# A two-layer graph network on one core: the inverse root of the degrees is taken by ScalarE, from VectorE's inverse counts, straight into the output rows

## What is computed

```python
h = jnp.maximum(_layernorm(x), 0.0)                   # x is 100000 x 128
neigh = h[dst] @ W_neigh.T + b_neigh                  # edge_index = (src, dst), 125000 edges
agg, count = segment_sum(neigh, src), clip(segment_sum(ones, src), 1)
x = x + h @ W_self.T + b_self + agg / count[:, None]  # layer one
h = jnp.maximum(_layernorm(x), 0.0)
deg = segment_sum(ones, dst)
dis = where(deg > 0, deg ** -0.5, 0)
x = x + relu(segment_sum(h[src] * (dis[src] * dis[dst])[:, None], dst))   # layer two
```

## Time and profile before

| | |
|---|---|
| time, median of 3 runs | 1208.86 us (1208.85, 1208.86, 1210.57) |
| profiled execution: span from first to last instruction | 1206.2 us |
| busy share of the span | PE 71%, PEld 65%, DVE 86%, ACT 88%, POOL 73% |
| layer one | from the first gather at about 28 us to the last store, issued at 717.7 us |
| layer two | from its first gather at 721.6 us to the end |
| mean granted TensorE clock | 0.779 |

### The profile page before, as it was taken

One profiled execution on the slowest core, in us unless ns is written; L12 is line 12 of the kernel. 1 busy time (PEld: TensorE's weight loads), 2 busy tenths in 40 slices (PEclk: granted clock), 3 DMA queues, 4 the chain that ended last, 5 costly groups with the idle time before them and its releaser, 6 DMA issues.

```text
span 1206.2 us, 30367 instructions
## 1 busy us (share of the span) xinstructions
PE 856.0 (71%) x9408; PEld 782.6 (65%) x9408; DVE 1042.0 (86%) x2896; ACT 1059.9 (88%) x2774; POOL 874.6 (73%) x1145
## 2 busy tenths in 40 slices
PE   1389999999999999999899972444444444444444
PEld 1378999998989998899899971343343433334334
DVE  7789999988989999999898845888888888888886
ACT  2489999998999999999899955888888888888886
POOL 4777777777777777777777507777777777777771
PEclk6699999999999999999999995555555555555555
DMA  5336667666766676677667435888888889888884
GB/s 206 116 85 200 200 211 212 189 193 203 207 193 196 206 212 188 198 204 213 179 205 210 143 115 185 255 262 272 267 265 280 259 268 275 264 283 256 263 280 185
DMA packets 82230, 259.38 MB, mean 215 GB/s; under 512 B 19986, under 2 KB 20356, under 8 KB 82116
## 3 DMA queue, kind: packets, MB, share of 16 engines
q1 hardware_dynamic: 58948, 210.86, 55.1%
q0 software_dynamic: 22400, 46.91, 14.5%
q10 hardware_dynamic: 768, 0.20, 0.1%
HBM read 152.93 MB, written 104.37 MB: 213 GB/s over the span
## 4 chain that ended last, share of the span: by engine, by line
POOL 48%; issue 25%; PE 9%; ACT 7%; DVE 6%; DMA 3%; POOLq 2%; ACTq 0%; DVEq 0%
POOL X L678 39%; ACT work L788 4%; POOL work L631 3%; POOL work L635 3%; PE p_O L962 2%; PE p_O L974 2%; DMA X<-in_x,IDX 2%; DVE ST L1397 2%; POOL work L615 2%; PE p_T L937 1%; PE p_T L912 1%; DVE area L1459 1%; POOL factor L651 1%; ACT area L803 1%; ACT p_O L788 1%
## 5 line engine op out<-in xcount | busy, mean ns | idle before, releaser
L788 ACT ACTIVATE work<-X,shift,scale 128x128 f32<-128x128 f32 x1323 | 546.9, 512 | 2.0 <-DVE shift L1434 1.8
L678 POOL DMA_INDIRECT X<-in_x,IDX x392 | 389.4, 993 | 128.2 <-issue 100.7
L1397 DVE BATCH_NORM_STATS2 ST<-X 128x6 f32<-128x256 f32 x1176 | 408.6, 414 | 37.6 <-DMA X<-in_x,IDX 35.6
L1025 PE MATMUL p_O<-work 32*128 32x128 f32 x1984 | 205.3, 435 | 223.9 <-POOL work L619 142.7
L678 POOL DMA_INDIRECT X<-x_table,IDX x294 | 286.0, 973 | 93.3 <-issue 90.5
L1025 PEld LDWEIGHTS p_O<-work 32*128 32x128 f32 x1984 | 178.0, 323 | 244.4 <-issue 186.2
L788 ACT ACTIVATE p_O<-X,shift,scale 128x128 f32<-128x128 f32 x496 | 201.3, 444 | 27.0 <-DVE area L1490 24.1
L962 PE MATMUL p_O<-wnT,area 128*128 128x128 f32 x1568 | 216.9, 282 | 2.9 <-DVE area L1459 2.9
L974 PEld LDWEIGHTS p_O<-wsT,area 128*128 128x128 f32 x1568 | 206.8, 192 | 7.5
L974 PE MATMUL p_O<-wsT,area 128*128 128x128 f32 x1568 | 207.4, 275 | 0.0
L962 PEld LDWEIGHTS p_O<-wnT,area 128*128 128x128 f32 x1568 | 191.6, 193 | 3.9 <-DVE area L1459 3.8
(11 more groups left out here) (177 smaller groups left out, 1163.3 us busy)
## 6 DMA issues: line engine op xcount, KB each, us to landing
x_table<-area SPq DMA_DIRECT2D x98, 528.0 KB
X<-x_table SPq DMA_DIRECT2D x98, 528.0 KB
X<-in_x SPq DMA_DIRECT2D x98, 512.0 KB, 4.6
out_x<-area SPq DMA_DIRECT2D x98, 512.0 KB, 5.9
X<-in_x,IDX POOLq DMA_INDIRECT x392
X<-x_table,IDX POOLq DMA_INDIRECT x294
moved<-held SPq DMA_DIRECT2D x32, 12.2 KB
es<-in_src SPq DMA_DIRECT2D x1, 488.5 KB, 3.4
```

Source lines behind the costliest of these rows:

```text
L678: nc.gpsimd.indirect_dma_start(got(s)[:, k, 0:w], None, table, bass.IndirectOffsetOnAxis(ap=IDX[:, s, k:k + 1], axis=0)).then_inc(gathered ...
L788: last = nc.scalar.activation(o, row(l, s, r), ACT.Relu, bias=shift[:, s, r:r + 1], scale=scale[:, s, r:r + 1])
L1025: ends[half] = nc.tensor.matmul(outs1[p][g][:, c], SEL[1][q, p, part_of, :], H[1][q, p, draw, :], start=False, stop=(half == 1 and part_of ...
L1397: last = V.bn_stats(ST[:, s, r:r + 2, :].rearrange("p r k -> p (r k)"), pair.rearrange("p r c -> p c r"))
```

## The change

DVE's inverse counts `rc` are kept for five blocks instead of two, and `sdeg` is gone. ACT, at the place in its step where the root of the counts was, now takes the root of `rc` of a block two blocks older, and writes it into column 128 of that block's output rows (`dis`, semaphore `dis_ready`). For this it waits for the store of two blocks before. PE's `aggregate` now waits for DVE's `counts_read`. DVE's second inverse is gone; SP waits for DVE's last L1459 and for `dis_ready`.

```diff
-        rc = sb("rc", [P, 2, BT])
-        sdeg = sb("sdeg", [P, HT, BT])
+        rc = sb("rc", [P, HT, BT])
...
-                sp.wait_ge(y_ready[l], place(l, turn, old)[0] + 1)
+                if l == 0:
+                    sp.wait_ge(prod_used[1], old + 1)
+                    sp.wait_ge(dis_ready, old + 1)
+                else:
+                    sp.wait_ge(y_ready, place(l, turn, old)[0] + 1)
...
-            def root_degrees(turn, off):
+            def dis(turn, off):
+
                 i, _, _ = place(0, turn, off)
                 act.wait_ge(counts_read, i + 1)
-                nc.scalar.activation(sdeg[:, off % HT, :], p_c[:, 0:BT], ACT.Sqrt).then_inc(sdeg_ready, 1)
+                if not first(i, HR[0]):
+                    act.wait_ge(stored[0][off % HR[0]], stores_before(0, turn, off) * 16)
+                nc.scalar.activation(made(0, off % HR[0])[:, :, D].rearrange("p (g j) -> p g j", g=2),
+                                     rc[:, off % HT, :].rearrange("p (j g) -> p g j", g=2), ACT.Sqrt
+                                     ).then_inc(dis_ready, 1)
...
-                if there(0, turn, off - 1):
-                    root_degrees(turn, off - 1)
+                if there(0, turn, off - 3):
+                    dis(turn, off - 3)
...
-                    pe.wait_ge(sdeg_ready, i)
+                    pe.wait_ge(counts_read, i)
...
-                    pe.wait_ge(sdeg_ready, NB)
+                    pe.wait_ge(counts_read, NB)
...
-            def dis(turn, off):
-
-                i, s, _ = place(0, turn, off)
-                dve.wait_ge(sdeg_ready, i + 1)
-                V.reciprocal(made(0, off % HR[0])[:, :, D].rearrange("p (g j) -> p g j", g=2),
-                             sdeg[:, off % HT, :].rearrange("p (j g) -> p g j", g=2)).then_inc(y_ready[0], 1)
...
                 dve.wait_ge(aT_ps, i + 1)
-                V.reciprocal(rc[:, off % 2, :], p_c[:, 0:BT]).then_inc(counts_read, 1)
+                if not first(i, HT):
+                    dve.wait_ge(dis_ready, i - HT + 1)
+                V.reciprocal(rc[:, off % HT, :], p_c[:, 0:BT]).then_inc(counts_read, 1)
...
                     added(turn, off - 3, 1)
-                    dis(turn, off - 3)
```

More of the change, by code:

```diff
@@ L161, in schedule, with stores_before @@
             step(0, off)
+    def stores_before(l, turn, off):
+        return turn * (RING[l] // HR[l]) + off // HR[l]
     def group_of(i):
@@ L414, in gnn @@
         h_ready = [sem(f"h_ready{l}") for l in range(2)]
-        y_ready = [sem(f"y_ready{l}") for l in range(2)]
+        y_ready = sem("y_ready1")
         hT_ps = sem("hT_in_psum")
@@ L420, in gnn @@
         counts_read = sem("counts_read")
-        sdeg_ready = sem("sqrt_deg_ready")
+        dis_ready = sem("dis_columns_ready")
         n_ready = [sem(f"neighbour_products_ready{g}") for g in range(2)]
@@ L777, in normalise @@
                         if l == 1:
-                            act.wait_ge(y_ready[1], i - HR[1] + 1)
+                            act.wait_ge(y_ready, i - HR[1] + 1)
                 if l == 1 and first(i, HR[1]) and i == HR[1] - 1:
@@ L1448, in scaled @@
                 bank = out0(off, g)[:, :].rearrange("p (a b) -> p a b", a=GT)
-                V.tensor_tensor(bank, bank, rc[:, off % 2, g:BT:2].rearrange("p (a b) -> p a b", b=1).to_broadcast([P, GT, P]),
+                V.tensor_tensor(bank, bank, rc[:, off % HT, g:BT:2].rearrange("p (a b) -> p a b", b=1).to_broadcast([P, GT, P]),
                                 ALU.mult).then_inc(n_scaled[g], 1)
@@ L1460, in added @@
                                 own(0, s)[:, GT * g:GT * g + GT, 0:D], ALU.add).then_inc(prod_used[g], 1)
-            def dis(turn, off):
-                i, s, _ = place(0, turn, off)
-                dve.wait_ge(sdeg_ready, i + 1)
-                V.reciprocal(made(0, off % HR[0])[:, :, D].rearrange("p (g j) -> p g j", g=2),
-                             sdeg[:, off % HT, :].rearrange("p (j g) -> p g j", g=2)).then_inc(y_ready[0], 1)
-            def stores_before(l, turn, off):
-                return turn * (RING[l] // HR[l]) + off // HR[l]
             def inverse_counts(turn, off):
@@ L1492, in finish1 @@
                 if g == 1:
-                    last.then_inc(y_ready[1], 1)
+                    last.then_inc(y_ready, 1)
             def step0(turn, off):
```

## The result

The changed kernel takes 1212.13 us (median of 20 runs, 1209.15 to 1214.5) against 1208.26 us for the kernel before (20 runs, 1206.54 to 1211.95). The ratio is 1.0026, 95% interval 1.0019 to 1.0034: slower, by 2.3 to 4.1 us. I had forecast no measurable change.

The account below looks back on a forecast made before the run. POOL's pace, 6.72 us a block, was taken to bound layer one, hiding most of the change; 0.43 us off its end took the median from 1208.86 to 1208.4 us, range 1205 to 1211.7.

Parts of the forecast that it names:

- the rival that came true: Layer one: DVE's new phase puts L1418 on POOL's L631; six more blocks cost 2.6 us, typical loss 3 us; chance 0.12.
- The sign that I had set for being wrong: POOL, layer one: L631's mean or L678's gaps changing by over 25 ns a block, or ACT waiting for stores.
- the sum: End of layer one: 0.21 + 0.11 + 0.11 = 0.43 us off, nothing else on the path.
- PE's start 0.14 us behind the inverse's end: Last wait before POOL's last gathers end: PE follows DVE's inverse by the same 0.14 us as it followed ACT's root.
- the 0.21: End of layer one: PE waits for DVE's inverse instead of ACT's root and starts 0.21 us sooner.
- the first 0.11 us: Behind the last gathered rows that hold DVE up: without the second inverse, the inverse of rows 8 comes 0.11 us sooner.
- the second 0.11: Very end of layer one: no inverse behind the last L1459, so the last store goes out 0.11 us sooner.
- ACT's 15.5 us in front of the root: Layer one: ACT's wait for DVE's inverse, 17 places; forecast to vanish there, most of it idle elsewhere on ACT.
- the 0.5 us that I expected: End of layer one: ACT's last root waits for a store, delaying the `DISL` DMAs some 0.5 us; cost 0.
- The inverse, put at 0.11 us a block: DVE, steady part: dropping the second inverse saves 0.11 us a block, hidden; 10.8 us for all 98 were DVE the bound.
- ACT's root out of SBUF: ACT, steady part: the root reading SBUF costs 0.13 us more a block, hidden under POOL's pace.
- the inverse's removal gives POOL nothing: Port rule: L1418 and L1434 contend with POOL, the removed inverse never did, so its removal alone gives POOL nothing.

Follow-up runs that it names:

- e5: Changed kernel plus one DVE inverse of `rc` into a spare tile where the removed one was; 1211.72 us, ratio 1.0000 to the kernel before.
- e6: Changed kernel with the old waits back: ACT's root for the newest counts, PE's `aggregate` for ACT's root; 1214.65 us, ratio 1.0026 to the kernel before.
- e7: Changed kernel with POOL's normalising instructions moved between the second and third gather, one step earlier; 1193.71 us, ratio 0.9858 to the kernel before.
- e8: Kernel before with POOL's normalising instructions moved between the second and third gather, one step earlier; 1190.39 us, ratio 0.983 to the unmoved kernel before.

## Why the prediction was wrong

**The step that failed** is in the rival that came true, where I argued against it: "A DVE that comes early is held there, into the phase that leaves L631 alone, and would be held 0.11 us longer." I had read one held shift, 0.52 us ahead of L631, and took the hold to catch any earlier one. It catches none that starts more than 0.66 us ahead and misses some from 0.63 on (in e5 one at 0.59), and that is where the removed inverse puts it. A shift that is not held lets the comparison start 0.25 us or more sooner, on POOL's first normalising instruction, which then takes up to 0.6 us longer. The rows that would have told this were in the trace of before: its 17 stretched blocks (0.89 us at 389.35) are those in which the shift started 0.62 to 1.08 us ahead and was not held. The rival's mechanism and size were right: it took six more met blocks as enough to decide, and the trace has seven more (17 to 24, 3.5 us), and its typical loss of 3 us stands against 0.26% of 1208.26, 3.1 us. The argument that kept its chance at 0.12 was the mistake. The sign that I had set for being wrong, over 25 ns in L631's mean, came true with 40. The range ended at 1211.7, 0.4 us below the measured median, because it took in half of that case only.

That the inverse's removal is the cause is shown: with an inverse in its place the ratio is 1.0000 (e5), and on the same chip without one it is 1.0026 even with the old waits (e6). That it acts through the overlap of L1430 with L638 is read from the traces (means of 0.526, 0.565, 0.529 us and 17, 24, 17 stretched blocks where the ratio is 1, 1.0026, 1.0000; 0.040 x 98 = 3.9 us). The run that would have removed the overlap where POOL is the bound is missing, so that link is argued, not shown. e6 fits it less well: 0.546 us, but its profiled execution took 1209.59 us, 5.1 us below its median. About 1.1 of the 5.09 us by which the last gather is later are not between the two normalising instructions at all.

**What held.** POOL was still the bound and never waited for L638's inputs before 678 us. The end of layer one became 0.39 us shorter where the sum had 0.43, in part by luck. PE's start 0.14 us behind the inverse's end came true as 679.71 - (679.37 + 0.19) = 0.15:

```profile
679.37 0.19 DVE L1480 RECIPROCAL rc<-p_c 128x8 f32<-128x8 f32 x1
...
679.71 0.49 PE L949 MATMUL p_T<-work 64*128 64x128 f32 x4 [0.83 <-DVE rc L1480]
```

But this last wait lies in another block, 2.84 us before POOL's last gather and not 9.36, so the 0.21 and the first 0.11 us can't be checked one by one. What the sum put at 0.32 us up to the last output rows measured 5.09 - 4.67 = 0.42. From these rows to the store's issue it was 722.24 - 721.52 = 0.72 us instead of 0.83, the second 0.11. And the store took 2.89 us to land instead of 2.75, which the sum did not have:

```profile
722.24 2.89 DMA x_table<-area
```

ACT's 15.5 us in front of the root are gone. In their place ACT's wait for PE in front of the copy L810 (L803 before) grew from 6.8 to 11.7 us, and that for DVE's statistics in front of L767 from 17.3 to 19.9. PE waited 11.7 us in 19 places for DVE's inverse, where it had waited 9.2 in 14 for ACT's root, so ahead of POOL's last gathers these waits did not get shorter. The lines in the changed kernel:

```profile
ACT area L810 <- PE p_c L959: 11.7, 12, 4.8
...
PE p_T L949 <- DVE rc L1480: 11.7, 19, 0.8
```

ACT waited for a store once, in the end, 5.16 us, and `DISL` was copied 719.10 - 713.53 = 5.57 us later, 0.48 beyond POOL's 5.09: the 0.5 us that I expected, and layer two's gathers did not move by it.

**Two terms of the steady part were mis-sized**, and both were hidden there. The inverse, put at 0.11 us a block, is worth 0.07 at the comparison and 0.063 in DVE's busy time. The other is ACT's root out of SBUF: ACT in order of time shows 0.11 us from it to the next instruction, where the earlier trace rows had 0.07.

```profile
671.05 0.23 ACT L818 ACTIVATE area<-rc 128x8 f32<-128x8 f32 x1
671.16 3.18 ACT L795 ACTIVATE work<-X,shift,scale 128x128 f32<-128x128 f32 x8
```

So 0.04 us more, not the 0.13 that I took from L760. The Trainium skill ("Perfetto Trace Analysis", Optimizing Scalar/DVE Operations) had given 0.04, and e7 against e8 agrees with 0.037 us a block. It shows as soon as POOL is quicker than ACT.

**On the port.** The Trainium skill ("SBUF — State Buffer", Who interferes with whom) has VectorE's instructions with two SBUF inputs contend with a GpSimd instruction that reads SBUF, and not those with at most one, outside VectorE's two-port modes. The trace agrees as to who contends, with 1.02 us for L638 under L1430. From it I concluded that the inverse's removal gives POOL nothing; but it is the schedule behind the inverse that meets POOL.

## What to carry to other kernels

An instruction that never touches the bounding engine can still place another one on it: before 0.1 us is cut from an engine with slack, list the offsets between its port-sharing instructions and those of the bound, and see how near to an edge they lie. Plan with the distribution over all blocks, not with the one block that looks well-behaved. And look at what the bounding engine's own queue does between two instructions: here moving its semaphore work behind a running DMA was worth 18 to 21 us, some five times what the change cost.

## What was unexpected of the hardware

A hold of the shift by POOL's gather has an edge: two shifts that start 0.63 us ahead of L638 took 0.48 and 0.22 us, and L638 then 0.45 and 1.02. In the traces of before, after, e5 and e6 both outcomes occur only 0.59 to 0.66 us ahead. Of the two instructions that meet, POOL's waits even where it started first: L638 at 384.25 took 1.02 us, and L1430, which came 0.11 us behind it, took its 0.68. POOL's next gather came 0.95 us behind a 0.54 us instruction and 0.97 us behind a 0.80 us one, so its queue works on in parallel. And the kernel before took 1211.51 us on one chip and 1353 to 1379 us on five others, with waits for something that the profile doesn't name.
